# Two clips of the last Newton pass move from DVE to POOL, and one pair's statistics move down in DVE's order

## The reference

```
for _ in range(3):
    scores = einsum('bhsd,hnd->bhsn', xi, K) * beta      # 256 memory slots
    w = entmax15(scores)
    xi = einsum('bhsn,hnd->bhsd', w, V)
out = xi @ Wo.T;  x = x + layernorm(out)
```

## Time and profile before

| | us |
|---|---|
| median of 3 runs | 1821.33 (1820.55 to 1825.54) |
| profiled execution | 1821.18, its span 1819.4 |

### The profile page before, as it was taken

The page is one execution under the profiler, slowest core; times in us unless marked ns, Lnnn a source line. Parts: engine busy times, 40 slices in busy tenths (PEclk is TensorE's granted clock), DMA queues, the critical chain, the costliest instruction groups (busy, mean ns, idle before and its releaser), DMA issues. The chain is left out here.

```text
span 1819.4 us, 25815 instructions
## 1 busy us (share of the span) xinstructions
PE 1564.8 (86%) x7434; PEld 1099.6 (60%) x7434; DVE 1361.7 (75%) x3568; ACT 1150.3 (63%) x2769; POOL 756.4 (42%) x2049
## 2 busy tenths in 40 slices
PE   5799999999857788887997789877779999999987
PEld 2545657465646667766776678666645556555554
DVE  6665757572359999999999999999644566766646
ACT  3333342412148999899998998899547565665630
POOL 3514224140136776777667776777410101001000
PEclk9799999998988989989998999899889999999989
DMA  5000000000110000000000000000000000000000
GB/s 230 1 1 1 1 1 1 1 1 0 55 57 1 1 1 1 1 1 1 1 1 1 1 1 1 1 1 1 1 0 1 1 1 1 1 13 1 13 1 23
DMA packets 6716, 19.21 MB, mean 11 GB/s; under 512 B 1072, under 2 KB 4144, under 8 KB 5296
## 3 DMA queue, kind: packets, MB, share of 16 engines
q1 hardware_dynamic: 6576, 17.58, 2.6%
HBM read 15.48 MB, written 2.10 MB: 10 GB/s over the span
## 5 line engine op out<-in xcount | busy, mean ns | idle before, releaser
L1361 DVE BATCH_NORM_STATS2 r_moments<-mem_arena 128x6 f32<-128x512 f32 x576 | 382.7, 683 | 4.4 <-ACT mem_arena L1649 4.3
L1649 ACT ACTIVATE mem_arena<-mem_arena,r_shift 128x256 f32<-128x256 f32 x792 | 351.2, 513 | 33.1 <-POOL r_shift L1554 33.1
L1717 PE MATMUL r_bank<-arena,r_wT 128*128 128x256 f32 x1024 | 228.4, 381 | 7.5 <-ACT mem_arena L1649 5.8
L1717 PEld LDWEIGHTS r_bank<-arena,r_wT 128*128 128x128 f32 x1024 | 192.0, 190 | 37.9 <-issue 13.1
L1734 PE MATMUL r_bank<-ident,mem_arena 128*128 128x128 f32 x576 | 107.9, 323 | 90.2 <-DVE mem_arena L1377 89.5
L1734 PEld LDWEIGHTS r_bank<-ident,mem_arena 128*128 128x128 f32 x576 | 81.9, 166 | 127.2 <-DVE mem_arena L1377 97.2
L1325 DVE MAX8 r_top<-r_bank 128x8 f32<-128x256 f32 x384 | 144.2, 416 | 14.5 <-PE r_bank L1717 14.0
L2275 ACT ACTIVATE arena<-arena,e_NM 128x512 f32<-128x512 f32 (+3 forms) x256 | 134.4, 559 | 29.2 <-DVE e_NM L1963 29.2
L1717 PE MATMUL r_bank<-arena,r_xnT 128*128 128x256 f32 x512 | 120.8, 396 | 19.9 <-ACT mem_arena L1649 19.1
L1963 DVE CUSTOM_DVE_ANT_0 arena<-e_banks,mask_q 128x512 f32<-128x512 f32 (+3 forms) x256 | 110.2, 485 | 29.7 <-PE e_banks L2480 29.3
L1361 DVE BATCH_NORM_STATS2 r_moments<-r_u 128x6 f32<-128x512 f32 x192 | 129.2, 684 | 2.8 <-ACT r_u L1649 2.6
(11 more groups left out here) (332 smaller groups left out, 3366.2 us busy)
## 6 DMA issues: line engine op xcount, KB each, us to landing
w<-in_w SPq DMA_DIRECT2D x3, 1024.0 KB, 14.3
out_x<-X SPq DMA_DIRECT2D x4, 512.0 KB, 2.9
X<-in_x SPq DMA_DIRECT2D x1, 1536.0 KB, 10.7
w_in<-in_w_in SPq DMA_DIRECT2D x1, 1156.0 KB, 6.5
mem_arena<-in_wq SPq DMA_DIRECT2D x1, 1024.0 KB, 17.1
mem_arena<-in_wo SPq DMA_DIRECT2D x1, 1024.0 KB, 20.9
gate<-in_gate SPq DMA_DIRECT2D x1, 1024.0 KB, 7.6
up<-in_up SPq DMA_DIRECT2D x1, 1024.0 KB, 9.6
```

Source lines behind the costliest of these rows:

```text
L1361: last = dve.bn_stats(moments[:, a.lane, 2 * p:2 * p + 2, :].rearrange("p two c -> p (two c)"), u[a.lane][:, 2 * p:2 * p + 2, :].rearrange ...
L1649: last = act.activation(u[a.lane][:, h, :], u[a.lane][:, h, :] if k else scores[:, h, :], ACT.Relu, bias=shift[:, a.lane, h:h + 1])
L1717: last = pe.matmul(scores[:, h, :], lhs, (G1 if a.first else G2)[:, h, i, :], start=i == 0, stop=i == 1)
```

## The change

The clips of heads 6 and 7 in pass 3 leave DVE's order. POOL gets the function `clip`, called for both heads directly behind `start` of a unit two younger, and ahead of the second moment of pass 3. The clips' semaphore is now counted up by POOL (`pool_clipped`). On DVE the statistics of pass 3, pair 3, don't follow those of pair 2; they stand behind the output statistics and the pass 0 statistics of pair 0 of a younger unit. All else keeps its place.

```diff
-DVE_CLIPS = ((), (), (), (3,))
+POOL_CLIPS = ((), (), (), (3,))
...
             def take_moments(a, k, *pairs):
...
-                    if p in DVE_CLIPS[k]:
-                        dve.wait_ge(dve_clipped[k], of_unit(a, len(DVE_CLIPS[k]), DVE_CLIPS[k].index(p) + 1))
+                    if p in POOL_CLIPS[k]:
+                        dve.wait_ge(pool_clipped[k], of_unit(a, len(POOL_CLIPS[k]), POOL_CLIPS[k].index(p) + 1))
...
@@ DVE, order of a slot
-                clip(Unit(n - 6), 3, 6)
                 take_moments(Unit(n - 6), 3, 1)
                 bound(Unit(n - 4))
-                clip(Unit(n - 6), 3, 7)
-                take_moments(Unit(n - 6), 3, 2, 3)
+                take_moments(Unit(n - 6), 3, 2)
                 out_stats(Unit(n - 8))
                 take_moments(Unit(n - 4), 0, 0)
+                take_moments(Unit(n - 6), 3, 3)
                 invert(Unit(n - 6), 3)
...
@@ POOL (the same function stood on DVE, with dve. and dve_clipped)
+            def clip(a, k, *heads):
+                if not a.live:
+                    return
+                pool.wait_ge(shift_ready[k - 1], of_unit(a))
+                for h in heads:
+                    last = pool.tensor_scalar(u[a.lane][:, h, :], u[a.lane][:, h, :], shift[:, a.lane, h:h + 1], 0.0,
+                                             ALU.add, ALU.max)
+                    if h % 2:
+                        last.then_inc(pool_clipped[k], 1)
...
@@ POOL, order of a slot
                 newton(Unit(n - 4), 1)
                 start(Unit(n - 3))
+                clip(Unit(n - 5), 3, 6, 7)
                 second_moment(Unit(n - 5), 3)
```

More of the change, by code:

```diff
@@ L1262, in memory_block @@
             "clear_ready", "troot_ready", "back_ready", "bound_ready", "start_ready"))
-        clipped, dve_clipped, moments_ready, inv_ready, s2_ready, root_ready, shift_ready = (
+        clipped, pool_clipped, moments_ready, inv_ready, s2_ready, root_ready, shift_ready = (
             [sem(f"{n}{k}") for k in range(PASSES)] for n in (
-                "clipped", "dve_clipped", "moments_ready", "inv_ready", "s2_ready", "root_ready", "shift_ready"))
+                "clipped", "pool_clipped", "moments_ready", "inv_ready", "s2_ready", "root_ready", "shift_ready"))
         dve_weights, pool_weights, wT_in_psum, wT_ready = (sem(n) for n in (
@@ L1341, in bound @@
                 dve.tensor_reduce(neg8[:, a.lane], back[:, a.lane], AX.X, ALU.max, negate=True).then_inc(bound_ready, 1)
[L1343 to L1351, removed]
             def take_moments(a, k, *pairs):
@@ L1356, in take_moments @@
                 for p in pairs:
-                    if p in DVE_CLIPS[k]:
-                        dve.wait_ge(dve_clipped[k], of_unit(a, len(DVE_CLIPS[k]), DVE_CLIPS[k].index(p) + 1))
+                    if p in POOL_CLIPS[k]:
+                        dve.wait_ge(pool_clipped[k], of_unit(a, len(POOL_CLIPS[k]), POOL_CLIPS[k].index(p) + 1))
                     else:
-                        dve.wait_ge(clipped[k], of_unit(a, NPAIR - len(DVE_CLIPS[k]), p + 1 - sum(q < p for q in DVE_CLIPS[k])))
+                        dve.wait_ge(clipped[k], of_unit(a, NPAIR - len(POOL_CLIPS[k]), p + 1 - sum(q < p for q in POOL_CLIPS[k])))
                     last = dve.bn_stats(moments[:, a.lane, 2 * p:2 * p + 2, :].rearrange("p two c -> p (two c)"),
```

## The result

The changed kernel takes 1885.22 us (median of 4 runs, 1882.01 to 1887.72) against 1821.42 (1820.55 to 1825.54) for the kernel before. The ratio is 1.0345, 95% interval 1.0322 to 1.0367: 64 us slower.

The account below looks back on a forecast made before the run. One loop through POOL, ACT and DVE sets the slot, not DVE's busy share; 12 output slots at 1.12, 12 rstd at 1.56, 20 plain at 1.34, plus 0.2, give 59.1; tail 5, in all +64: 1885 us, range 1871 to 1893.

Parts of the forecast that it names:

- Rival 3: DVE's busy share decides; its 0.52 us of removed clips counts in each slot: 1798 us; chance 0.03.
- rival 4: Waits are half hidden by unseen slack: +0.5 to +1 us a slot, 1845 to 1868 us; chance 0.07.
- Pass 0 pair 0: DVE's statistics wait for ACT's first two clips, starting 1.20 us after slot start (before: 1.31); no loss by itself.
- Pass 0 pair 1, 1.20 late: DVE's statistics, after POOL's clips and the inverse, start 3.23 us after slot start instead of 2.03.
- Root, head 5, pass 0 pair 2 at S+4.67: ACT's late root delays head 5's clip; DVE's pair 2 starts 4.67 us after slot start instead of 3.20: 1.47 late.
- Slots with rstd: 12 slots where POOL also makes a tile's rstd and is the bound: +1.56 us each.
- The gain at the bound: At slot end, head 6's missing clip lets the bound come earlier: 0.13 us taken, at most 0.18.
- Slots with output, +1.12: 12 slots with a tile's output: DVE's output norm waits for POOL's later output rstd, +1.12 us each, no bound gain.
- rival 1: PE's longer hole leaves its clock at 1.2 GHz for the scores' beginning: 20 to 30 us more, about 1910; chance 0.08.
- I take nothing for it: PE's hole before the transposes grows from 2.63 to about 4.1 us; no cost was counted.
- Rival 2: POOL's clips take DVE's 0.35 us: +0.63 in 33 slots, about +0.4 in 12 with output, some 1849 us; chance 0.04.
- The tail, 5: Units 45 to 47 after the last slot add 1.5, about 1.4 and 2.4 us, together 5.

Follow-up runs that it names:

- order-only kernel: Kernel before, clips still on DVE, only the statistics of pass 3 pair 3 moved behind pass 0 pair 0: 1855.52 us, ratio 1.0187.
- kernel with the early clip of head 6: Kernel before, with DVE's clip of head 6 moved ahead of the clear of the room in all slots: 1819.91 us, ratio 0.9988.
- kernel with four idle products: Changed kernel, with 4 idle matmuls on PE ahead of each unit's first transposes: 1882.19 us, ratio 1.0322.
- kernel with short clips: Changed kernel, with POOL's two clips cut to 32 of 256 columns each, part of the computation missing: 1854.55 us, ratio 1.0190.

## Why the prediction was right, step by step

**The loop, not the shares.** Shown. Taking the clips away altogether brought 11 us, not 23, and putting them on an engine with 31% of idle time cost 64. Rival 3 (faster) falls with both. So does rival 4 (half of the waits hidden, 1845 to 1868): each further microsecond of clips cost a full one.

**The wait for POOL's clips.** Predicted: pair 3 at S+2.52; measured: S+2.51 (1267.73). The clips took 2.25 together (predicted 2.26); no work of DVE's beside them slowed them (96 clips, all of 1.14).

**Pass 0 pair 0, placed too early.** Predicted S+1.20; measured S+1.34 (1266.56), so that the waits were 0.81 for ACT and 0.47 for POOL's clips and not 0.6 each. ACT's first pass 0 clip starts at S+0.49 and not S+0.29. In ACT's order a clip that waits for POOL's Newton shift stands ahead of it (1265.29), and that shift now lies 0.16 ahead of the start where it was 0.38. It cost nothing here, since pair 3 waits longer anyway; but it means that where ACT is what DVE waits for, as with short clips, an earlier start gives nothing.

**Pass 0 pair 1, 1.20 late.** Measured S+3.37 (1268.59), so 1.34. The term that was short is the inverse: behind a statistics on whose end it waits directly it starts 0.74 after it and the next starts 0.12 after that, 0.86 and not 0.72. Before, one other statistics stood between the two. It cost nothing here, because pair 2 was held by ACT's clip of head 5.

**Root, head 5, pass 0 pair 2 at S+4.67.** Measured: POOL's sum ends at S+4.00 (1269.02 and 0.20), the root starts at S+4.04, pair 2 at S+4.64. So ACT's wait was 1.24 and not 1.5, and DVE's before pair 2 was 0.10 and not 0.3. POOL's second moment of pass 0 at S+6.69 against S+6.70, its running sums at S+10.83: +1.47 on the earlier trace rows, as predicted. The order-only kernel shows the split: 1.06 of pair 3's delay of 1.80 comes with the order, the rest with POOL's length.

**Slots with rstd.** POOL, from the start at 617.42:

```profile
617.42 0.20 POOL L1525 TENSOR_TENSOR r_shift<-r_neg,r_top 128x8 f32<-128x8 f32 x1
...
622.53 0.20 POOL L1540 TENSOR_TENSOR r_spread<-r_root,r_s 128x8 f32<-128x8 f32 x1
...
624.29 0.23 POOL L1531 TENSOR_TENSOR r_spread<-r_moments,r_inv_n 128x8 f32<-128x8 f32 x1
```

The second moment of pass 0 (624.29) is at S+6.87, predicted 6.92, with no wait: POOL is the bound there, as said. In five of the twelve it is at 7.05 or later; in four of these a weight of POOL's took 1.31 and not 1.14, with one of DVE's weights beside it. The excess of the prediction in plain and rstd slots is the next term.

**The gain at the bound, mis-sized.** I took 0.13 with 0.18 as its end. From the running sums to the next start was 6.32 (1235.56 to 1241.88) and is 6.02 (1276.05 to 1282.07): 0.30. A wait of 0.18 went, as said. The rest, 0.12, comes with an instruction of POOL's that I held fixed. Before the change, beside DVE's clip of head 6 (1240.43 to 1240.78), it was:

```profile
1240.49 0.35 POOL L1545 TENSOR_TENSOR r_s<-r_spread,r_meansq 128x8 f32<-128x8 f32 x1
```

After, it is 0.20 (1280.94). The kernel with the early clip of head 6 shows that it is the clip: in its plain slots

```profile
1238.12 0.20 POOL L1545 TENSOR_TENSOR r_s<-r_spread,r_meansq 128x8 f32<-128x8 f32 x1
```

and in a slot in which the clip now runs at 591.40, another POOL instruction is the slow one:

```profile
591.42 0.36 POOL L1543 TENSOR_TENSOR r_meansq<-r_moments 128x8 f32<-128x8 f32 x1
591.92 0.23 POOL L1545 TENSOR_TENSOR r_s<-r_spread,r_meansq 128x8 f32<-128x8 f32 x1
```

0.36 for a sum that takes 0.20 otherwise. So the change gave back 0.17 a slot that I had not counted, about 5 us in 33 slots. The instruction is at 0.34 to 0.38 in all 45 slots before, those with output too, for which I had taken no gain: there the stretch from the sums to the start went from 6.32 to between 6.04 and 6.25 in eleven of twelve. The Trainium skill (SBUF — State Buffer, Who interferes with whom) says that of a DVE `tensor_scalar` in a 2-port mode and a GpSimd instruction, the one that is issued first has the shared ports for its whole length, and the other waits. The trace agrees: in all 45 slots before, the sum ends 0.06 after the clip that started ahead of it. Which mode DVE's clip runs in, no run here shows.

**Slots with output, +1.12.** Measured +1.30, and it takes two errors to come that near. Up to the running sums the term is right in eight of the twelve: 10.89 before, 11.98 after, +1.09. The gain behind them (above) leaves 0.8 to 1.0: slots of 18.02 to 18.23 for 17.22. DVE's waits there (the first row is of the slot of 18.93, the other two of the one after it):

```profile
758.59 0.43 DVE L66 BATCH_NORM_STATS2 r_ostats<-r_bank 128x6 f32<-128x256 f32 x1 [1.71 <-PE r_bank L1751]
...
777.80 0.70 DVE L1351 BATCH_NORM_STATS2 r_moments<-mem_arena 128x6 f32<-128x512 f32 x1 [0.43 <-POOL mem_arena L1558]
...
780.17 0.54 DVE L1380 TENSOR_SCALAR r_onorm<-r_bank,r_omv,r_ors 128x256 f32<-128x256 f32 x1 [0.26 <-POOL r_ors L1569]
```

DVE waits for POOL's clips (777.80), and 0.26 for POOL's output rstd (780.17). But four of the twelve are 18.9 to 19.3, and in them DVE waits 1.7 to 1.9 for PE's output (758.59). That is rival 1, in another place than I put it. PE ahead of that slot:

```profile
752.35 0.82 PE L1734 MATMUL r_bank<-ident,r_u 128*128 128x128 f32 x4 [2.12 <-DVE r_u L1367]
752.96 3.42 PE L1751 MATMUL r_bank<-arena,r_wT 128*128 128x256 f32 x8
```

and its windows (PEclk is the number before the last two):

```profile
751.00:752.00 1.00, 0.00 (x0) 0.00 (x0) 1.00 (x3) 1.00 (x4) 0.85 (x3) 1.00 0.00 0
...
753.60:754.60 1.00, 1.00 (x3) 0.80 (x3) 0.64 (x1) 1.00 (x3) 0.84 (x4) 0.50 0.00 0
757.60:758.60 1.00, 1.00 (x7) 0.85 (x6) 0.01 (x1) 1.00 (x4) 1.00 (x2) 1.00 0.00 0
```

A hole of 2.12 where it was 1.05, then a granted clock of 0.5, so 1.2 GHz, and the eight instructions of output products take 3.42 for 1.89. In the changed kernel's plain slots, for which I weighed this rival, PE has time to spare and the clock costs nothing; in output slots PE was busy 16.0 to 16.2 of 17.2 us before (13 in the last of each four). I looked at the hole of the plain slot and not at that of the output slot, which has no reserve behind it. So "I take nothing for it" is the step of the prediction that failed: the kernel with four idle products shows that it cost 0.34 a slot, 4 us. Without it the output slots are 18.17, +0.96.

**Rival 2** (clips as short as DVE's, about 1849): its premise is false, the clips took 1139 ns each; its arithmetic is 6 us low, the kernel with short clips took 1855: plain slots +0.62 (0.63 forecast), output slots +0.46 (0.4), but those with rstd +0.96, for which it also had 0.63. The price of 32 columns is 394 ns, so 224 further columns cost 745 ns, 3.3 ns each. The rule of the Trainium skill (GPSIMD Engine Reference, Engine selection), roughly line rate for one input, doesn't hold for this operation, which takes 1139 ns on POOL and 345 on DVE.

**The tail, 5.** Its terms make 5.3; measured 6.2. Unit 46 and unit 47 in DVE's timeline:

```profile
1354.04 0.65 DVE L1351 BATCH_NORM_STATS2 r_moments<-r_u 128x6 f32<-128x512 f32 x1
1355.56 0.54 DVE L1380 TENSOR_SCALAR r_onorm<-r_bank,r_omv,r_ors 128x256 f32<-128x256 f32 x1 [0.87 <-POOL r_ors L1569]
...
1367.56 0.70 DVE L1351 BATCH_NORM_STATS2 r_moments<-r_u 128x6 f32<-128x512 f32 x1 [1.01 <-POOL r_u L1558]
```

The 0.87 for output rstd is that of unit 46's slot, behind second moments that stood behind DVE's late pair. The 1.01 is unit 47's wait for POOL's clips, which had the first batch's norms ahead of them, as predicted. From the last start to this statistics 4.4 were added. The other 1.8 come behind it, most of them from PE's clock again:

```profile
1373.24 0.63 PE L1734 MATMUL r_bank<-ident,r_u 128*128 128x128 f32 x4 [3.09 <-DVE r_u L1367]
1373.70 3.45 PE L1751 MATMUL r_bank<-arena,r_wT 128*128 128x256 f32 x8
```

The hole before was 1.43, and the products behind it took 1.89. With four idle products the tail is 58.2 where it is 59.5 here.

In all, the mechanism is right, and the hit on the number (1885 for 1885.22) is in part luck. The sum had 59.1 for 55.2 in the slots, with 6 too much in plain and rstd slots against 2 too little in output slots; it had 5 for 6.2 in the tail, and nothing for the 5 us outside the two. The range of 1871 to 1893 would have held each of these errors alone.

## What to carry to other kernels

When engines run in order and one loop goes through all of them, an idle hole is worth something only if what is put in comes out before somebody waits for it. Count where the moved work ends, not how long the engine idles: here a hole of 1.23 took 2.25 of work, and 1.02 of it stuck out, with a root and a queue behind it. An instruction that seems to do no more than wait its turn may be what fills an engine's time until its next input comes; moving it one later cost 34 us here with no work added.

## What the runs showed of the hardware that was not expected

- DVE's `tensor_scalar` (128x256 fp32, 345 ns) beside POOL's `tensor_tensor` of 128x8: the POOL instruction takes 0.34 to 0.38 for 0.20. POOL's `tensor_scalar` of 128x256 takes 1.31 for 1.14 beside such a DVE instruction in four slots, and 1.40 beside DVE's `tensor_tensor` of 128x256 in all twelve output slots of the changed kernel.
- POOL's `tensor_scalar` with two operations and a scalar per partition costs 394 ns at 32 columns and 1139 ns at 256.
- The changed kernel has seven holes of 2.1 on PE in its output slots. Behind four of them the granted clock was 0.5 for more than 3 us, behind the other three it stayed at 1.0. Which it hits, no run here settles.
